# A decoder layer of 16 batch pairs: the order around the cross scores, who applies the cross mask, and when the next rows' statistics are taken

## What is computed

```python
x = x + attn(layernorm(x), Wqa, Wqb, Wkva, Wkvb, Wout, bout)     # causal, rope, softmax(q k^T / 4)
x = x + xattn(layernorm(x), ctx, ctx, mask, wq, bq, ..., wo, bo) # softmax(where(mask == 0, -1e9, q k^T / 4))
x = x + ffn(layernorm(x), w1, b1, w2, b2)                        # relu, float_quantize, matmul, float_quantize
```

## Time and profile before

| | us |
|---|---|
| median of the runs (3) | 1729.31 |
| the profiled execution: its own time | 1726.77 |
| its span, first to last instruction | 1725.1 |
| PE busy | 1617.5 (94% of the span) |
| VectorE (DVE) busy | 1159.0 (67%) |
| ScalarE (ACT) busy | 1116.1 (65%) |
| GpSimd (POOL) busy | 753.5 (44%) |
| mean granted TensorE clock | 0.982 |

### The profile page before, as it was taken

One profiled execution on the slowest core, in us unless ns is written; L12 is line 12 of the kernel. 1 busy time (PEld: TensorE's weight loads), 2 busy tenths in 40 slices (PEclk: granted clock), 3 DMA queues, 4 the chain that ended last, 5 costly groups with the idle time before them and its releaser, 6 DMA issues.

```text
span 1725.1 us, 33722 instructions
## 1 busy us (share of the span) xinstructions
PE 1617.5 (94%) x11950; PEld 973.6 (56%) x11950; DVE 1159.0 (67%) x1736; ACT 1116.1 (65%) x1733; POOL 753.5 (44%) x1010
## 2 busy tenths in 40 slices
PE   3879999999999999999999999999999999999988
PEld 2445556656555565655656555665655556565555
DVE  4557576685857758586676858668585775857573
ACT  4455675766668566665856567576666856666574
POOL 2252344644345553444545334464434555344410
PEclk7979999999999999999999999999999999999999
DMA  7473453754547374553845546375454737454420
GB/s 182 59 99 70 68 85 65 103 95 64 96 60 107 68 96 90 75 84 57 119 72 81 94 66 89 65 103 95 64 96 60 106 68 96 90 75 73 62 40 13
DMA packets 106238, 140.17 MB, mean 81 GB/s; under 512 B 12385, under 2 KB 74242, under 8 KB 105954
## 3 DMA queue, kind: packets, MB, share of 16 engines
q1 hardware_dynamic: 103090, 130.96, 51.0%
q0 software_dynamic: 2352, 8.26, 1.5%
q10 hardware_dynamic: 768, 0.57, 0.1%
HBM read 21.29 MB, written 8.39 MB: 17 GB/s over the span
## 4 chain that ended last, share of the span: by engine, by line
PE 75%; DMA 9%; ACT 6%; DVE 4%; issue 3%; POOL 2%; SPq 1%; DVEq 0%; ACTq 0%; POOLq 0%
PE o_pair L1457 14%; PE score L1418 8%; PE small L1543 7%; DMA Q<-negT 5%; PE small L1577 5%; PE o_pair L1288 5%; PE small L1288 4%; PE score L1395 3%; PE small L1304 3%; PE score L1341 3%; DVE negmax L1021 2%; PE score L1376 2%; PE small L1470 2%; DMA sums<-o_sb 2%; PE score L1400 2%
## 5 line engine op out<-in xcount | busy, mean ns | idle before, releaser
L1021 DVE TENSOR_REDUCE negmax<-score 128x4 f32<-128x1024 f32 (+1 forms) x384 | 456.9, 1216 | 73.4 <-PE score L1376 47.0
L780 ACT ACTIVATE P<-score 128x1024 f32<-128x1024 f32 x448 | 446.4, 1026 | 74.6 <-PE score L1418 26.4
L1053 DVE TENSOR_TENSOR P<-P,cross_bound 128x1024 f32<-128x1024 f32 x192 | 230.8, 1250 | 88.6 <-ACT P L780 88.5
L1457 PE MATMUL o_pair<-P,V 128*32 128x256 f32 (+1 forms) x4096 | 280.0, 362 | 2.6 <-DVE P L1053 2.4
L828 ACT ACTIVATE score<-cross_q 128x1024 f32<-128x1024 bf16 x192 | 196.3, 1023 | 46.4 <-DVE negmax L1021 42.9
L1418 PE MATMUL score<-Q,K 99*128 99x256 bf16 x1024 | 152.3, 276 | 25.9 <-DMA Q<-negT 24.8
L1457 PEld LDWEIGHTS o_pair<-P,V 128*32 128x32 f32 x4096 | 87.8, 108 | 134.6 <-issue 73.4
L1577 PE MATMUL small<-xnT,w 128*128 128x256 f32 x600 | 157.6, 381 | 0.0
L1418 PEld LDWEIGHTS score<-Q,K 99*128 99x128 bf16 x1024 | 83.7, 98 | 125.7 <-ACT P L780 61.7
L558 POOL TENSOR_TENSOR x<-x,ffn 128x1024 f32<-128x1024 f32 x15 | 32.8, 2189 | 268.9 <-DVE negmax L1021 268.9
L1376 PE MATMUL score<-K,Q 96*128 96x256 bf16 x768 | 121.0, 282 | 9.9 <-ACT score L828 5.4
(11 more groups left out here) (202 smaller groups left out, 3049.4 us busy)
## 6 DMA issues: line engine op xcount, KB each, us to landing
K<-k2p SPq DMA_DIRECT2D x96, 256.0 KB, 6.2
Q<-q2p SPq DMA_DIRECT2D x192, 128.0 KB, 5.2
Q<-q1p SPq DMA_DIRECT2D x90, 256.0 KB, 6.7
x_in<-in_x SPq DMA_DIRECT2D x16, 512.0 KB, 5.3
ctxT<-in_ctx SPq DMA_DIRECT2D x16, 512.0 KB, 7.1
k2f<-q1f SPq DMA_DIRECT2D x32, 256.0 KB, 6.3
inT<-o_sb SPq DMA_DIRECT2D x60, 128.0 KB
o<-inverse SPq DMA_DIRECT2D x60, 128.0 KB
```

The costliest lines, as they stand in the source:

```text
L780: A.activation(P[:, t % 4, :], score[b][:, :, :], ACT.Exp, scale=SCALE).then_inc(score_free[b], 1)
L1021: V.tensor_reduce(negmax[:, k, h:h + 1024 // w], s.rearrange("p (h w) -> p h w", w=w), AX.X, ALU.max, negate=True).then_inc(score_free[b], 1)
L1053: V.tensor_tensor(p, p, cross_bound[:, t % 2, :].unsqueeze(1).broadcast_to([128, 4, SEQ]), ALU.min).then_inc(probs_masked[1], 1)
L1457: last = T.matmul(o_ps[ob][32 * j:32 * j + 32, SEQ * gg + q0:SEQ * gg + SEQ], v, p, start=s == 0, stop=end, tile_position=(0, 32 * j), ski ...
```

## The change

Five places move, none of them changes what is computed.

- **Mask of the cross tiles.** Tiles 7 and 11 of E2 lose the two mask matmuls and are capped by VectorE instead; tiles 3 and 15 stay with TensorE. So 14 of 16 tiles go through VectorE (12 before).
- **SP.** `put_neg(st, 1, 0)` goes ahead of `put_part("q1", 0, i + 1)`.
- **ScalarE.** In S2, `cut_first` goes ahead of the premask of tile 10, `cut_second` from 11 to 10, and `maxima` from after tile 13 to after tile 12.
- **GpSimd.** `cut_rest(1, i, 0)` goes ahead of the last sum of the k1 rotation, `cut_third` ahead of the first part of q1; `inverse_root(0, i + 1)` goes from early in S1 to just ahead of the masks of E1.
- **VectorE.** The statistics of the next rows go from E2 to after the last row maxima of S1 (in `body(0)`: from after tile 8 to after tile 11).

```diff
-        BOUNDED = (N1 - 2, 3 * UNITS)
+        MASK_ADDED = (3, N2 - 1)
+        BOUNDED = (N1 - 2, N2 - len(MASK_ADDED))
         def bounded(a, t):
-            u, s = t // TPU[a], t % TPU[a]
-            if a == 0:
-                return t - (t > 2) if t not in (2, N1 - 1) else None
-            return 3 * u + s if s < 3 else None
+            added = (2, N1 - 1) if a == 0 else MASK_ADDED
+            return t - sum(m < t for m in added) if t not in added else None
...
                     sp.dma_start(ctxT[:, :, :], ctx_v[i + 1]).then_inc(ctx_loaded, 16)
+                put_neg(st, 1, 0)
+                if nxt:
                     put_part("q1", 0, i + 1)
-                put_neg(st, 1, 0)
-                if nxt:
                     put_part("k1", 0, i + 1)
...
                 cut_third(0, i, 0)
-                if nxt:
-                    inverse_root(0, i + 1)
                 keys_rest(st, i)
...
                 cut_third(0, i, 1)
+                if nxt:
+                    inverse_root(0, i + 1)
                 for t in range(N1):
...
                     rope_products("k1", cosk, sink, k1s, i + 1)
+                cut_rest(1, i, 0)
+                if nxt:
                     rope_sum("k1", k1s, i + 1)
+                cut_third(1, i, 0)
+                if nxt:
                     part("q1", 0, whole, part1, i + 1)
-                cut_rest(1, i, 0)
-                cut_third(1, i, 0)
...
                 for t in range(3, N2):
+                    if t == 10:
+                        cut_first(1, i, 0)
                     if t not in PE_MASKED:
                         premask(i, t)
                     if prev and t in EVICT_AFTER:
                         hidden(st, [3 + EVICT_AFTER.index(t)])
                     if t == 10:
-                        cut_first(1, i, 0)
-                    if t == 11:
                         cut_second(1, i, 0)
-                    if t == 13:
+                    if t == 12:
                         maxima(st, 1, 0)
...
-                    if t == 11 and nxt:
-                        dve.wait_ge(x_loaded, 16 * (i + 2))
-                        block_stats(0, x_in, range(3))
-                if nxt:
-                    norm_stats(0, x_in, i + 1, range(3, NBLK))
...
                 for t in range(N1):
                     row_max(0, i, t)
...
-                    if not prev and t == 8:
-                        dve.wait_ge(x_loaded, 16 * (i + 2))
-                        norm_stats(0, x_in, i + 1)
+                if nxt:
+                    dve.wait_ge(x_loaded, 16 * (i + 2))
+                    norm_stats(0, x_in, i + 1)
```

More of the change, by code:

```diff
@@ L460, in body @@
                     sp.dma_start(ctxT[:, :, :], ctx_v[i + 1]).then_inc(ctx_loaded, 16)
-                    put_part("q1", 0, i + 1)
                 put_neg(st, 1, 0)
                 if nxt:
+                    put_part("q1", 0, i + 1)
                     put_part("k1", 0, i + 1)
@@ L646, in body @@
                     rope_products("k1", cosk, sink, k1s, i + 1)
+                cut_rest(1, i, 0)
+                if nxt:
                     rope_sum("k1", k1s, i + 1)
-                    part("q1", 0, whole, part1, i + 1)
-                cut_rest(1, i, 0)
                 cut_third(1, i, 0)
                 if nxt:
+                    part("q1", 0, whole, part1, i + 1)
                     rest("q1", i + 1)
@@ L1164, in _, with cross_bounds @@
             V.tensor_tensor(q1p[:, 2, :, SEQ:TOK], q[1], q1p[:, 1, :, SEQ:TOK], ALU.subtract).then_inc(part3["q1"], 1)
-            def cross_bounds(st, g, i=None, nxt=False):
+            def cross_bounds(st, g, i=None):
                 for t in range(N2):
@@ L1183, in body @@
                 if prev:
-                    cross_bounds(st, i - 1, i, nxt)
+                    cross_bounds(st, i - 1, i)
                 for t in range(N1):
```

## The result

| | before | changed |
|---|---|---|
| median of the runs, us | 1728.9 (1727.0 to 1732.7, 4 runs) | 1772.4 (1771.8 to 1784.0, 4 runs) |
| ratio of the times | | 1.027, 95% interval 1.023 to 1.030 |
| profiled execution, us (span) | 1726.8 (1725.1) | 1772.1 (1770.5) |
| mean granted clock | 0.982 | 0.973 |
| a body of the loop, us | 102.4 | 105.65 (8 of 12) or 106.3 (4 of 12) |

The change costs 45.4 us of span where 15.3 were forecast, and the time lies above the range. The lines that follow are of the changed kernel's seventh body; the rows of before that they answer to are named beside them.

A forecast was written before the change was run, and what follows sets the result against it. Prediction: PE's waits on DMA in E2 bound the kernel, one at tile 0 and the next close behind. Terms 3.2 + 16.8 + 0 - 4.7 = +15.3 on 1726.8, 1742.1; median 1744.6 us, range 1708 to 1760.

The forecast's parts named there:

- tile 0's wait: Start of E2: PE's wait of 1.64 us for the maxima goes, since they are issued ahead of the large transfers.
- tile 8's wait: Middle of E2: batch 1's maxima land behind 1.6 MB on SP's queue; PE waits 2.7 us, tile 8 starts 0.66 later.
- clock: TensorE in E2: idle 2.7 us drops the clock in nine bodies of ten, 1.33 us each, +16.8 in 14; bounds 0, +21.
- statistics: After S1, ahead of the residual: moving them there costs 0, bounds 0 and 0.3 us a body; leaving E2 gains nothing.
- The upper bound, 758.6: E2: latest start of tile 8, if the maxima land as far behind the last transfer as that lands later; 757.65 taken.
- The low end: E2: tile 8 starts at 756.5 if the maxima need only engines through early, such as three of 16.
- GpSimd's inverse root: Moved ahead of the masks for E1: costs nothing, as PE's first product there comes over a us after the transposition.
- The price of eleven caps: E2: VectorE's caps at 1.17 against PE's 1.11 cost at most 0.6 us a body if nothing else held PE.
- Outside the 14: First group -2.8 us, first body -1.6, end piece -0.3 (between -0.9 and +3.0); together -4.7.
- the second rival: E2: the wait at tile 8 is there but the clock holds; 1727.8 us, or 1711.7 at the low end; chance 0.22.
- The first: Rival, E2: all gained, batch 1's maxima not held, tile 8 at 754.92; 1689.6 us (1698 with caps); chance 0.20.
- The third: Rival, after S1: statistics beside GpSimd's additions hold PE too, 1 us a body; 1759 us with the clock; chance 0.05.

The follow-up runs named there:

- e13_split_old_masks: e5_split with the masks of tiles 7 and 11 back on TensorE; 1708.8 us, ratio 0.988.
- e12_act_queue_held: Changed kernel with batch 1's maxima on ScalarE's queue and SP held until ScalarE has copied them, so only 1.6 MB are ahead; 1759.6 us, ratio 1.017.
- e3_masks_alone: Kernel before with only the masks of tiles 7 and 11 moved from TensorE to VectorE's caps; 1720.8 us, ratio 0.996.
- e4_stats_alone: Kernel before with only the statistics of the next rows and GpSimd's inverse root moved; 1734.5 us, ratio 1.0039.
- e1_queue_back: Changed kernel with SP's order put back alone: 768 KB of q1 ahead of batch 0's maxima; 1740.1 us, ratio 1.0075.
- e5_split: Changed kernel with the second pieces of q1 and k1 (640 KB) issued behind batch 1's maxima; 1697.1 us, ratio 0.982.
- e6_filled: Changed kernel with 28 extra matmuls into tile 8's score bank ahead of its wait, overwritten by tile 8; 1747.9 us, ratio 1.0115.
- e2_queue_alone: Kernel before with SP's new order and nothing else; 1793.2 us, ratio 1.038.
- e8_pool_back: e1_queue_back with GpSimd's order of S2 undone too, q1's first piece made ahead of the two cuts; 1729.6 us, ratio 1.001.

## Why the prediction was wrong

Direction and mechanism were right, and the forecast case came: tile 0 has no wait, tile 8 waits for the maxima, the clock falls in E2. The size was not: a body lost 3.46 us where 1.43 were forecast. By terms, us a body:

| term | forecast | measured |
|---|---|---|
| tile 0's wait | -1.64 | -1.44 |
| mask of tile 7 | -0.43 | -0.36 |
| tile 8's wait | +2.73 | +3.74 |
| mask of tile 11 | -0.43 | -0.43 |
| clock | +1.20 | +1.70 |
| statistics | 0 | +0.21 |
| rest of the middle and S2 | 0 | +0.04 |
| sum | +1.43 | +3.46 |

The last mask is that of the earlier trace rows, confirmed by e13_split_old_masks. The clock is the stretch from tile 8 to S1's transposition, 23.0 on average, less its 21.74 before, plus the mask of 0.43.

**Tile 8's wait** is the step that failed. "I take 757.65, nearest to the last landing with a little for their own 24 KB": counted from S2's transposition, the last large transfer was forecast at +18.5 and landed at +18.8, so the traffic was sized nearly right. The little, up to the start of tile 8, was 0.35 and is 1.4: it makes half of the 2.03 us a body that were missed. It could have been read from the trace of before. The three pieces ahead of tile 0's maxima take, each in its own window of issue:
```profile
Q<-q1p SPq DMA_DIRECT2D x1, 256.0 KB, 4.5
...
Q<-q1p SPq DMA_DIRECT2D x1, 256.0 KB, 6.2
...
Q<-q1p SPq DMA_DIRECT2D x1, 256.0 KB, 7.8
```
The third is issued at 738.55 and lands at 746.4. PE starts on the maxima at 747.42, 1.0 behind. The 6.6 us of the last large transfer were the median of two; alone it takes 6.8:
```profile
K<-k1p SPq DMA_DIRECT2D x1, 64.0 KB, 6.8
```
With both the wait would have been forecast at 3.6 (753.9 + 3.6 + 1.0 - 754.92). The upper bound, 758.6, had that microsecond in it, and tile 8 came 0.3 beyond, counted in the same way; between the bounds the wrong value was taken. All upper bounds together (16.5, 21 and 4.2, less 4.7) give 1766 as a median, and the range had stopped at 1760. The low end, which the prediction drew from the Trainium skill (DMA: Bandwidth & Descriptors, "Why a DMA increments its semaphore by 16 and not by 1"), did not come: where the maxima run alone (at 754.5 in the kernel before), 0.15 to 0.20 of the 16 engines are busy, so about three do carry them, as that section says, but they were not through early in any run.

**The clock**: "about nine bodies of ten" at 1.33 each. It fell in all 13 bodies with the full wait. With a wait of the forecast length it would have been about right: in e12_act_queue_held (2.7 us) it fell in nine of twelve, and cost 1.47. The size was low too. The three us at half speed were counted in whole microseconds; the neighbours on either side are partly slow, and together they make 3.4:
```profile
1644.00:1645.00 1.00, 1.00 (x7) 0.73 (x7) 0.97 (x1) 0.00 (x0) 0.00 (x0) 0.92 1.13 115
...
1648.00:1649.00 1.00, 1.00 (x6) 0.61 (x5) 0.25 (x1) 0.63 (x2) 0.00 (x0) 0.87 0.12 13
```
By the forecast's own working 3.4 us cost 1.5, as measured in eight bodies of twelve. In the other four the clock falls during the wait, and PE works 4.8 us at half speed and loses 2.1.

**Statistics**: "Cost 0, with next to no cover", bounds 0 and 0.3: 0.21, by the residual that delays the transposition's bank. They take 2.11 where 1.92 was read from the earlier trace rows. The other half of the step, that taking them out of E2 "gains nothing there", was wrong once the masks move: e3_masks_alone shows 0.39 a body lost by their staying. GpSimd's inverse root, "so nothing", costs 0.33 at a mask of E1 (e4_stats_alone); that the table shows only 0.04 is luck, since the earlier cuts give 0.30 back, which the forecast had not counted either. The price of eleven caps, "at most 0.6", had the right size and the wrong place: not on the products in E2 but on the self scores' banks.

**Tile 0**: gone as forecast. Of its 1.64, 0.17 come back at once: the first eight matmuls take 1.22 where after a wait they took 1.05.

**ScalarE's and GpSimd's cuts**: the prediction priced only what they bring forward (the maxima). GpSimd's order also sends q1 out 1.0 us later, which is part of the 3.6 forecast by another way (SP's order made q1 wait for the maxima), so it cost nothing here; e1_queue_back shows it where the order doesn't hide it.

**Outside the 14**: -4.7 forecast, -2.1 measured; the end piece gave +1.8 for -0.3, within its bounds but not by the caps. A product does wait longer for a cap there (1.76 for 1.33), which only eats up a mask's 0.43. 1.6 of the 1.8 are the clock's: behind the same idle stretch of 2.38 us that had cost nothing, it falls in the changed kernel, and the same eight matmuls take, before and changed,
```profile
1698.70 1.97 PE L1543 MATMUL small<-wo,inT 128*128 128x256 f32 x8
```
```profile
1742.72 3.34 PE L1538 MATMUL small<-wo,inT 128*128 128x256 f32 x8
```
Of the fifteen traces of this case twelve lose the clock behind this stretch. So the case on which the second rival leaned was the rarer one.

**Rivals.** The first (all gained, 1689.6) did not come, but its time nearly did, in e5_split (1697.1), once 640 KB less were ahead. The second (the wait is there, the clock holds) is e6_filled. The third needed 1 us a body from GpSimd's additions; e4_stats_alone shows 0.5 for the statistics and the inverse root together. The mean clock came out at 0.973 as forecast, but it is a poor witness: e5_split has 0.980 without a fall in any E2 of the loop, since the start and the end of the program weigh in.

## What to carry to other kernels

When a small transfer that someone waits for is moved ahead of large ones, ask at once which small one is next behind them, and count the bytes that lie between; moving 640 KB behind it turned 1772 into 1697. Here 24 KB in 48 rows landed about a microsecond behind the last transfer ahead of them, and another queue did not help them past. And an idle stretch of PE of over 2 us is to be priced with the clock that it takes down, in the kernel with the new wait and not only in that of before.

## What the runs showed of the hardware

**Queues.** 24 KB issued on ScalarE's or GpSimd's own queue did not move until what SP had issued earlier was through: with 2.4 MB ahead (two runs) their first packets moved over 8 us after issue; with 1.6 MB ahead, on ScalarE's queue, they landed after 6.9 us, for 7.25 on SP's queue. The Trainium skill (DMA: Bandwidth & Descriptors, "Queues, rings and completion order") says that a DMA engine takes turns between the queues it has work for; by that, one would expect the maxima to pass. These runs don't show it: with 16 engines at a share of 1.0 to 1.15 their packets kept the order of issue. Whether that order is kept in the engines or ahead of them no run here tells. The Trainium skill (DMA: Bandwidth & Descriptors, "Issuing engines are not separate DMA queues") says that spreading transfers over issuing engines saves only issue time; with that they agree.

**The clock after an idle stretch.** Ahead of a tile of E2 in full bodies, and in the last row once in each trace, in the end piece; the granted clock went from 1.00 (2.4 GHz) to 0.50 (1.2 GHz):

| run | idle, us | stretches | fell | lost each, us |
|---|---|---|---|---|
| e6_filled | 0.4 to 0.5 | 13 | 0 | |
| e3_masks_alone | 1.6 | 12 | 0 | |
| e1_queue_back | 2.35 to 2.47 | 13 | 3 | 1.7 |
| e12_act_queue_held | 2.69 to 2.77 | 12 | 9 | 1.5 |
| e2_queue_alone | 2.83 to 2.98 | 12 | 12 | 1.5 to 2.9 |
| changed | 3.65 to 3.78 | 12 | 12 | 1.5 or 2.1 |
| end piece of all fifteen | 2.38 to 2.39 | 15 | 12 | 1.4 to 1.7 |

These cases don't fit a rule by the length of one stretch: the end piece against e1_queue_back, with stretches of nearly one length; the second bodies of the changed kernel and of e3_masks_alone, which lost the clock after 1.84 and 2.11 us; and e8_pool_back, where it fell after idle pieces of under 0.7 us each, in four of 13 bodies.
